# Layer 0's recurrence in seven small VectorE instructions a step instead of six, with the growth kept apart from its inverse

## The chip, the cores and the metric

The kernel runs on one core of a Trainium2 chip. The metric is the device time of one execution in microseconds. All data is float32.

## What is computed

The kernel computes a four-layer model on x of 8 sequences of 512 tokens and 256 channels. Of it, only the first part matters here. Layer 0 normalises x, forms keys, values and gates by three projections, and runs a recurrence over the 512 tokens for each of 8 x 256 channels:

```
def step(carry, kv_t):
    aa, bb, pp = carry
    kk, vv = kv_t
    uu_kk = u + kk
    p = jnp.maximum(pp, uu_kk)
    e1 = jnp.exp(pp - p)
    e2 = jnp.exp(uu_kk - p)
    y = (e1 * aa + e2 * vv) / (e1 * bb + e2)
    ...
    pp_n = pu + jnp.log(bb_n)
```

Beside it stands a mixture of 16 experts on the same normalised x: every expert's output, silu(gate) times up, projected down, is weighted by a router's column and added to the residual. The recurrence's denominators depend on the step before; the experts depend on nothing in it.

## The kernel before

The program is a sequence of blocks, each with one instruction stream for every engine and a barrier at its ends. Layer 0 has three: `layer0_project`, `layer0_experts` and `layer0_mix`.

`layer0_project` goes over the 8 sequences: normalisation, projections, routing, the shared expert. ScalarE writes the exponentials of the decays into `scan`, a tile that stays for all of layer 0. It has T + 2 places of time, two slots each, and 16 columns (two channel blocks times 8 sequences). Slot 0 of place t+1 first holds a decay d and is overwritten in the recurrence by the state q; slot 1 of place t+1 holds the inverse of a clamped ratio of the step before.

`layer0_experts` runs two things on the same engines at once. The experts' work is cut into 128 units, 16 experts times 8 sequences. For a unit TensorE multiplies up (`ps_gu`, L577), ScalarE forms `silu_g` (L564) and copies `up_rows` (L565), GpSimd multiplies the two into `hidden` (L553), TensorE multiplies down (`ps_y`, L586), and VectorE adds `ps_y`, times the column of `comb`, to the residual `x_res` (`combine`, L507). `ps_gu`, `hidden` and `ps_y` have two buffers each. TensorE's order is up of unit m+1, then down of unit m; the down waits for `hidden_ready` and for `y_free`, which VectorE's last half combine of two units before raises.

VectorE's stream interleaves the recurrence with the combines, four time steps a unit. A step before is: `recurrence` (L487), one SCALAR_TENSOR_TENSOR over both slots, new = (q + 1) * (d, inverse); the first half combine of a tile, 128 columns; a wait; the clamp of the ratio (L494, TENSOR_SCALAR); the product that writes q (L495); the second half combine; a wait; the reciprocal of the ratio into slot 1 of place t+2 (L501); a wait for that reciprocal. The semaphore `step` counts all four. The first combine of a unit waits for `down_done`. The units go as two without a combine, seven passes of a loop over `j` with 16 units written out in each (addresses of `scan` are computed in registers there), and a last 14 units with fixed addresses. In the profile the time of L487, L494, L495, L501 and L507 is that of these instructions, and the same lines under DVEq are register work of VectorE's sequencer.

`layer0_mix` reads q of all steps out of `scan`, with the time as the running index: `q_at` in GpSimd's two additions (L678, L679) and VectorE's product (L700).

Of the kernel before, what the change touches and what calls it, by code (L numbers as in the profile page):

```python
# [20 lines left out]
ALU = mybir.AluOpType  # L21
# [3 lines left out]
P = 128  # L25
B, T, D = 8, 512, 256
KD = D // P
# [3 lines left out]
ONE = 1  # L31
# [136 lines left out]
RATIO_MAX = 1e24  # L168


def layer0_project(nc, io, keep):


    with ExitStack() as stack:
# [85 lines left out]
        def _(dve):  # L260
# [5 lines left out]
            nc.vector.memset(scan[:, 0, 0, :], 0.0).then_inc(setup_done, 1)  # L266
            nc.vector.memset(scan[:, 1, 1, :], 1.0).then_inc(setup_done, 1)
# [63 lines left out]
        def _(act):  # L331
            act.wait_ge(cols_in, ONE + DMA)
            act.wait_ge(setup_done, ONE + 5)
# [30 lines left out]
            def decays(i):  # L364
                act.wait_ge(dk_ready, ONE + i + 1)
                for k in range(KD):
                    last = nc.scalar.activation(
                        scan[:, 1:T + 1, 0, bass.ds(B * k + i, 1)].rearrange("p t a -> p (t a)"), dk[:, k, :],
                        ACT.Exp, bias=cols[:, k, 3:4])
                last.then_inc(decayed, 1)  # L370
# [10 lines left out]
        def _(pe):  # L381
            pe.wait_ge(weights_in, ONE + 5 * DMA)
            pe.wait_ge(setup_done, ONE + 5)
# [58 lines left out]
def layer0_experts(nc, io, keep):  # L442
# [3 lines left out]
    with ExitStack() as stack:  # L446
# [8 lines left out]
        ratio = room.sb("ratio", KD * B)  # L455
# [8 lines left out]
        step = room.sem("step")  # L464
# [16 lines left out]
        def _(dve):  # L481
            dve.sem_inc(y_free, 2)

            def recurrence(t):


                nc.vector.scalar_tensor_tensor(  # L487
                    out=new[:], in0=scan[:, bass.ds(t, 1), 0, :].broadcast_to([P, 2, KD * B]), scalar=1.0,
                    in1=scan[:, bass.ds(t + 1, 1), :, :].rearrange("p a s c -> p (a s) c"),
                    op0=ALU.add, op1=ALU.mult).then_inc(step, 1)  # L490

            def recurrence_close(t):
                dve.wait_ge(step, ONE + 4 * t + 1)
                nc.vector.tensor_scalar(ratio[:], new[:, 0, :], 1.0, RATIO_MAX, ALU.max, ALU.min).then_inc(step, 1)  # L494
                nc.vector.scalar_tensor_tensor(  # L495
                    out=scan[:, bass.ds(t + 1, 1), 0, :].rearrange("p a c -> p (a c)"), in0=new[:, 0, :],
                    scalar=RATIO_MAX, in1=new[:, 1, :], op0=ALU.min, op1=ALU.mult).then_inc(step, 1)

            def recurrence_invert(t):
                dve.wait_ge(step, ONE + 4 * t + 3)  # L500
                nc.vector.reciprocal(scan[:, bass.ds(t + 2, 1), 1, :].rearrange("p a c -> p (a c)"),  # L501
                                     ratio[:]).then_inc(step, 1)
# [9 lines left out]
            def unit(j, m, with_sum):  # L512


                u = 2 * B * j + m
                for s in range(UNIT_STEPS):
                    t = UNIT_STEPS * u + s
                    recurrence(t)
                    if with_sum:
                        if s == 0:  # L520
                            dve.wait_ge(down_done, ONE + u + 1)
                        combine(m - 2, s, 2 * j + (m - 2) // B, 0)
                    recurrence_close(t)
                    if with_sum:
                        last = combine(m - 2, s, 2 * j + (m - 2) // B, 1)
                        if s == UNIT_STEPS - 1:
                            last.then_inc(y_free, 1)
                    recurrence_invert(t)
                    dve.wait_ge(step, ONE + 4 * t + 4)
# [78 lines left out]
def layer0_mix(nc, io, keep):  # L608
# [4 lines left out]
    with ExitStack() as stack:  # L613
# [38 lines left out]
        def q_at(i, k, first):  # L652
            return scan[:, first:first + T, 0, bass.ds(B * k + i, 1)].rearrange("p t a -> p (t a)")
# [2800 lines left out]
def build_program(nc, io):  # L3454
    with ExitStack() as stack:
# [9 lines left out]
        with ExitStack() as layer0:  # L3465
            room0 = Room(nc, layer0, "l0")
            keep.scan = room0.sb("scan", T + 2, 2, KD * B)
# [152 lines left out]
```

## Time and profile before

| | us |
|---|---|
| median of 3 timed runs | 4336.93 (4331.45 to 4337.49) |
| the profiled execution, its own time | 4330.87 |
| its span | 4329.1 |
| VectorE busy in the span | 2632.6 (61%) |
| TensorE busy in the span | 3557.8 (82%) |
| GpSimd busy in the span | 1320.7 (31%) |

The span is what lies between the first and the last instruction of the profiled execution. `layer0_experts` runs from about 199 to 973 us of it. Times below are counted from the span's start. In a timeline row come the start in us, the duration in us, the engine (DVE is VectorE, PE TensorE, ACT ScalarE, POOL GpSimd), the line and operation, what is written from what, the shape, the number of instructions merged, and in brackets the engine's idle time before it with what ended that.

### The profile page before, as it was taken

What the parts mean: (1) busy time and instruction counts of PE and PEld (TensorE: products, weight loads), DVE (VectorE), ACT (ScalarE), POOL (GpSimd) and SP (SyncE); (2) the same over time, 40 slices, a digit from 0 to 9 for tenths busy, and PEclk for the clock granted to TensorE, in tenths of its full rate; (3) what the DMA queues carried; (4) which work ended last, traced back from release to release, by engine and by line L of the source; (5) the groups of instructions that cost most, each with busy time, mean ns of one, the idle gap of its engine ahead of it and who ended that gap; (6) DMA issues with size and microseconds to landing.
All of it is one profiled execution on the core that took longest, in us unless ns stands there. A gap on an engine that the chain in (4) does not pass through costs nothing. (4 is left out here: it accounts for less than half of the span.)

```text
span 4329.1 us, 49464 instructions
## 1 busy us (share of the span) xinstructions
PE 3557.8 (82%) x15062; PEld 2035.1 (47%) x15062; DVE 2632.6 (61%) x6864; ACT 1266.9 (29%) x2471; POOL 1320.7 (31%) x787
## 2 busy tenths in 40 slices
PE   7898899895887999799999996899968745666665
PEld 4454555453564555444444454656544522333332
DVE  5588888898883444346666644122234537887885
ACT  4511111112223666244344432123213311111110
POOL 1021222221111544112112111320230038777872
PEclk9999999997998999999999987799979976777777
DMA  3100000001102000100000002122210010000000
GB/s 104 71 8 8 8 12 8 8 4 66 44 29 100 1 1 1 35 6 16 16 15 16 15 20 105 56 71 88 88 59 15 15 50 14 10 10 15 10 5 39
DMA packets 66796, 136.42 MB, mean 32 GB/s; under 512 B 8096, under 2 KB 40480, under 8 KB 65824
## 3 DMA queue, kind: packets, MB, share of 16 engines
q1 hardware_dynamic: 60448, 117.22, 8.0%
q0 software_dynamic: 6144, 16.79, 1.2%
q8 instruction: 91, 1.49, 0.1%
q14 instruction: 113, 0.93, 0.1%
HBM read 77.62 MB, written 56.36 MB: 31 GB/s over the span
## 5 line engine op out<-in xcount | busy, mean ns | idle before, releaser
L577 PE MATMUL p_ps_gu<-l0x_xnT_all,p_w 128*128 128x512 f32 x1024 | 465.3, 598 | 6.5 <-DMA p_w<-l_w 6.5
L507 DVE SCALAR_TENSOR_TENSOR all_x_res<-p_ps_y,l_comb,all_x_res 128x128 f32<-128x128 f32 (+1 forms) x1016 | 351.7, 347 | 12.6 <-PE p_ps_y L586 8.6
L553 POOL TENSOR_TENSOR p_hidden<-p_silu_g,p_up_rows 128x512 f32<-128x512 f32 x128 | 162.6, 1270 | 637.3 <-ACT p_up_rows L565 637.3
L1916 DVE CUSTOM_DVE_ANT_0 a_ps_s<-a_ps_s,a_hide_row,a_fmax 128x384 f32<-128x384 f32 (+3 forms) x512 | 249.3, 554 | 170.3 <-PE a_ps_s L1623 170.0
L586 PE MATMUL p_ps_y<-p_w,p_hidden 128*128 128x256 f32 x1024 | 257.2, 395 | 72.6 <-DVE all_x_res L507 72.4
L3134 POOL TENSOR_TENSOR b_prod<-b_q,b_kv 128x4096 f32<-128x4096 f32 x32 | 287.3, 9001 | 64.4 <-ACT b_kv L3328 50.2
L577 PEld LDWEIGHTS p_ps_gu<-l0x_xnT_all,p_w 128*128 128x128 f32 x1024 | 197.2, 193 | 201.1 <-issue 187.1
L3147 POOL TENSOR_TENSOR b_prod<-b_att,b_kv 128x4096 f32<-128x4096 f32 x32 | 281.4, 8806 | 16.7 <-ACT b_att L3338 12.1
L586 PEld LDWEIGHTS p_ps_y<-p_w,p_hidden 128*128 128x128 f32 x1024 | 190.4, 194 | 186.5 <-issue 132.1
L564 ACT ACTIVATE p_silu_g<-p_ps_gu 128x512 f32<-128x512 f32 x128 | 76.4, 597 | 613.2 <-PE p_ps_gu L577 613.2
L1828 POOL TENSOR_SCALAR_AFFINE_SELECT a_probs<-a_probs 128x512 f32<-128x512 f32 x128 | 79.9, 636 | 565.3 <-ACT a_probs L2105 565.3
L1124 POOL TENSOR_TENSOR a_probs<-a_probs,a_causal 128x512 f32<-128x512 f32 (+1 forms) x96 | 157.6, 1653 | 215.7 <-ACT a_probs L1353 215.7
L1353 ACT ACTIVATE a_probs<-a_ps_s 128x512 f32<-128x512 f32 (+1 forms) x384 | 170.7, 537 | 119.9 <-PE a_ps_s L993 119.9
L2105 ACT ACTIVATE a_probs<-a_ps_s 128x512 f32<-128x512 f32 (+1 forms) x384 | 171.8, 537 | 91.0 <-PE a_ps_s L1645 90.5
L487 DVE SCALAR_TENSOR_TENSOR p_new<-l_scan 128x32 f32 (+1 forms) x512 | 127.0, 248 | 101.8 <-DVE l_scan L501 31.4
L3436 PE MATMUL b_ps_kv<-b_w_e,b_hT 128*128 128x512 f32 x256 | 132.7, 651 | 57.3 <-DVE all_x_res L3276 57.3
L3436 PE MATMUL b_ps_e<-b_w_e,b_hT 128*128 128x512 f32 x256 | 146.7, 726 | 19.6 <-DVE all_x_res L3276 16.5
L494 DVE TENSOR_SCALAR p_ratio<-p_new 128x16 f32<-128x16 f32 x512 | 154.5, 302 | 1.8
L3178 DVE TENSOR_REDUCE b_att<-b_prod 128x256 f32<-128x4096 f32 x32 | 140.5, 4410 | 17.8 <-POOL b_prod L3134 17.8
L2307 PE MATMUL b_ps_y<-b_w_ff,b_gelu 128*128 128x256 f32 x512 | 123.4, 395 | 31.3 <-issue 30.3
L3191 DVE TENSOR_REDUCE b_y<-b_prod 128x256 f32<-128x4096 f32 x32 | 140.1, 4398 | 9.4 <-POOL b_prod L3147 9.4
L2295 PE MATMUL b_side<-b_hT,b_w_ff 128*128 128x512 f32 x256 | 128.9, 657 | 15.0 <-issue 13.1
(419 smaller groups left out, 7175.8 us busy)
## 6 DMA issues: line engine op xcount, KB each, us to landing
sorted_scratch<-all_zero SPq DMA_DIRECT2D x1, 9088.0 KB, 30.5
b_sorted_in<-sorted_scratch SPq DMA_DIRECT2D x17, 512.0 KB, 4.6
y_scratch<-b_y_out SPq DMA_DIRECT2D x17, 512.0 KB, 3.2
all_x_res<-x SPq DMA_DIRECT2D x8, 512.0 KB, 4.7
xn_scratch<-p_xn SPq DMA_DIRECT2D x8, 512.0 KB, 5.2
v_scratch<-p_v_sb SPq DMA_DIRECT2D x8, 512.0 KB, 2.6
r_scratch<-p_r_sb SPq DMA_DIRECT2D x8, 512.0 KB, 2.8
p_w<-l_w SPq DMA_DIRECT2D x16, 256.0 KB, 2.6
```

The costliest lines, as they stand in the source:

```text
L494: nc.vector.tensor_scalar(ratio[:], new[:, 0, :], 1.0, RATIO_MAX, ALU.max, ALU.min).then_inc(step, 1)
L507: return nc.vector.scalar_tensor_tensor(out=xb, in0=ps_y[m % 2][:, t, part], scalar=comb[:, TT * (m % B) + t, bass.ds(e, 1)], in1=xb, op0= ...
L553: nc.gpsimd.tensor_tensor(hidden[m % 2][:], silu_g[m % 2][:], up_rows[m % 2][:], ALU.mult).then_inc(hidden_ready, 1)
L577: last = nc.tensor.matmul(ps_gu[m % 2][:, half, :], w13[n][:, k, half * INTER0:(half + 1) * INTER0], xnT_all[:, k, (m % B) * T:(m % B + 1) ...
L586: last = nc.tensor.matmul(ps_y[m % 2][:, t, :], hidden[m % 2][:, t * P:(t + 1) * P], w2[n][:], start=True, stop=True)
L1124: nc.gpsimd.tensor_tensor(lead, lead, allowed, ALU.mult).then_inc(masked, 1)
L1353: nc.scalar.activation(probs[g % 2][:, j, T * part:T * part + PART_LEN[part]], ps_s[:, j, 0:PART_LEN[part]], ACT.Square, scale=HD ** -0.5) ...
L1916: last = nc.vector.tensor_tensor_reduce(out=there, in0=there, in1=hide_row[:, (TT - 1 - t) * P:], scale=HD ** -0.5, scalar=fmax[i % 2][:, ...
L2105: nc.scalar.activation(probs[:, j, T * part:T * part + PART_LEN[part]], ps_s[:, j, 0:PART_LEN[part]], ACT.Exp, scale=HD ** -0.5).then_inc( ...
L3134: nc.gpsimd.tensor_tensor(prod[t % 3][:].rearrange("p (h g d) -> p h g d", h=HEADS, g=HEADS), q[:, t, :].rearrange("p (h a d) -> p h a d", ...
L3147: nc.gpsimd.tensor_tensor(prod[(TT + t) % 3][:].rearrange("p (h d g) -> p h d g", h=HEADS, d=HD), att[:, t, :].rearrange("p (h a g) -> p h ...
L3436: last = nc.tensor.matmul(ps_e[n % 4][:], hT[1][:, k, t * P:(t + 1) * P], w_e[:, k, 2 * pair * D:2 * (pair + 1) * D], start=(k == 0), stop ...
```

## The change

The clamped ratio and slot 1 of `scan` go. `scan` has one slot a place, T + 1 places. Two small tiles take the rest: `new` keeps the growth and the numerator's partner, `share` keeps the growth's inverse and a bounded share. A step becomes: `grow` with two 16-wide SCALAR_TENSOR_TENSORs, new0 = (q + 1) * d and new1 = min(share0, 1) + share1; the first half combine; a wait for both; the reciprocal of new0 into share0; share1 = min(new0, 1) * new1; q = min(new0, RATIO_MAX) * new1; the second half combine; a wait for all five. The description also names GpSimd as keeper of the gate times up product; that product is GpSimd's in the kernel before and the diff doesn't touch it.

```diff
-            nc.vector.memset(scan[:, 0, 0, :], 0.0).then_inc(setup_done, 1)
-            nc.vector.memset(scan[:, 1, 1, :], 1.0).then_inc(setup_done, 1)
+            nc.vector.memset(scan[:, 0, :], 0.0).then_inc(setup_done, 1)
...
                     last = nc.scalar.activation(
-                        scan[:, 1:T + 1, 0, bass.ds(B * k + i, 1)].rearrange("p t a -> p (t a)"), dk[:, k, :],
+                        scan[:, 1:T + 1, bass.ds(B * k + i, 1)].rearrange("p t a -> p (t a)"), dk[:, k, :],
...
         new = room.sb("new", 2, KD * B)
-        ratio = room.sb("ratio", KD * B)
+        share = room.sb("share", 2, KD * B)
...
             dve.sem_inc(y_free, 2)
-
-            def recurrence(t):
-
-
+            nc.vector.memset(share[:, 0, :], 1.0).then_inc(share_set, 1)
+            nc.vector.memset(share[:, 1, :], 0.0).then_inc(share_set, 1)
+            dve.wait_ge(share_set, ONE + 2)
+
+            def grow(t):
+
+                q = scan[:, bass.ds(t, 1), :].rearrange("p a c -> p (a c)")
+                nc.vector.scalar_tensor_tensor(out=new[:, 0, :], in0=q, scalar=1.0,
+                                               in1=scan[:, bass.ds(t + 1, 1), :].rearrange("p a c -> p (a c)"),
+                                               op0=ALU.add, op1=ALU.mult).then_inc(step, 1)
+                nc.vector.scalar_tensor_tensor(out=new[:, 1, :], in0=share[:, 0, :], scalar=1.0, in1=share[:, 1, :],
+                                               op0=ALU.min, op1=ALU.add).then_inc(step, 1)
+
+            def settle(t):
+                dve.wait_ge(step, ONE + 5 * t + 2)
+                nc.vector.reciprocal(share[:, 0, :], new[:, 0, :]).then_inc(step, 1)
+                nc.vector.scalar_tensor_tensor(out=share[:, 1, :], in0=new[:, 0, :], scalar=1.0, in1=new[:, 1, :],
+                                               op0=ALU.min, op1=ALU.mult).then_inc(step, 1)
                 nc.vector.scalar_tensor_tensor(
-                    out=new[:], in0=scan[:, bass.ds(t, 1), 0, :].broadcast_to([P, 2, KD * B]), scalar=1.0,
-                    in1=scan[:, bass.ds(t + 1, 1), :, :].rearrange("p a s c -> p (a s) c"),
-                    op0=ALU.add, op1=ALU.mult).then_inc(step, 1)
-
-            def recurrence_close(t):
-                dve.wait_ge(step, ONE + 4 * t + 1)
-                nc.vector.tensor_scalar(ratio[:], new[:, 0, :], 1.0, RATIO_MAX, ALU.max, ALU.min).then_inc(step, 1)
-                nc.vector.scalar_tensor_tensor(
-                    out=scan[:, bass.ds(t + 1, 1), 0, :].rearrange("p a c -> p (a c)"), in0=new[:, 0, :],
+                    out=scan[:, bass.ds(t + 1, 1), :].rearrange("p a c -> p (a c)"), in0=new[:, 0, :],
                     scalar=RATIO_MAX, in1=new[:, 1, :], op0=ALU.min, op1=ALU.mult).then_inc(step, 1)
-
-            def recurrence_invert(t):
-                dve.wait_ge(step, ONE + 4 * t + 3)
-                nc.vector.reciprocal(scan[:, bass.ds(t + 2, 1), 1, :].rearrange("p a c -> p (a c)"),
-                                     ratio[:]).then_inc(step, 1)
...
                     t = UNIT_STEPS * u + s
-                    recurrence(t)
+                    grow(t)
                     if with_sum:
                         if s == 0:
                             dve.wait_ge(down_done, ONE + u + 1)
                         combine(m - 2, s, 2 * j + (m - 2) // B, 0)
-                    recurrence_close(t)
+                    settle(t)
                     if with_sum:
                         last = combine(m - 2, s, 2 * j + (m - 2) // B, 1)
                         if s == UNIT_STEPS - 1:
                             last.then_inc(y_free, 1)
-                    recurrence_invert(t)
-                    dve.wait_ge(step, ONE + 4 * t + 4)
+                    dve.wait_ge(step, ONE + 5 * t + 5)
...
         def q_at(i, k, first):
-            return scan[:, first:first + T, 0, bass.ds(B * k + i, 1)].rearrange("p t a -> p (t a)")
+            return scan[:, first:first + T, bass.ds(B * k + i, 1)].rearrange("p t a -> p (t a)")
...
-            keep.scan = room0.sb("scan", T + 2, 2, KD * B)
+            keep.scan = room0.sb("scan", T + 1, KD * B)
```

In `layer0_project` ScalarE and TensorE wait for four set-up steps instead of five.

## Rows read from the trace of the kernel before

**Rows 1.** Windows: busy us (x instructions) of PE, PEld, DVE, ACT, POOL; clock; DMA

```profile
600.00:700.00 100.00, 89.66 (x264) 49.56 (x263) 83.87 (x397) 19.53 (x35) 20.44 (x17) 0.98 0.03 9
```

**Rows 2.** Waits of TensorE and VectorE, 206 to 970 us: total, times, longest

```profile
PE p_ps_y L586 <- DVE all_x_res L507: 72.4, 91, 3.3
...
DVE all_x_res L507 <- PE p_ps_y L586: 6.5, 1, 6.5
```

**Rows 3.** Timeline of VectorE: the first instruction of two passes of the loop

```profile
605.57 0.19 DVE L487 SCALAR_TENSOR_TENSOR p_new<-l_scan 128x32 f32 x1 [3.12 <-issue]
...
702.59 0.19 DVE L487 SCALAR_TENSOR_TENSOR p_new<-l_scan 128x32 f32 x1 [3.12 <-issue]
```

**Rows 4.** Timeline of GpSimd, early in that pass

```profile
624.60 1.26 POOL L553 TENSOR_TENSOR p_hidden<-p_silu_g,p_up_rows 128x512 f32<-128x512 f32 x1 [3.89 <-ACT p_up_rows L565]
629.76 1.26 POOL L553 TENSOR_TENSOR p_hidden<-p_silu_g,p_up_rows 128x512 f32<-128x512 f32 x1 [3.90 <-ACT p_up_rows L565]
```

**Rows 5.** Timeline of VectorE: the last step of a unit and the next unit's start

```profile
655.68 0.24 DVE L501 RECIPROCAL l_scan<-p_ratio 128x16 f32 x1
656.07 0.19 DVE L487 SCALAR_TENSOR_TENSOR p_new<-l_scan 128x32 f32 x1
656.21 0.35 DVE L507 SCALAR_TENSOR_TENSOR all_x_res<-p_ps_y,l_comb,all_x_res 128x128 f32<-128x128 f32 x1
656.48 0.16 DVE L494 TENSOR_SCALAR p_ratio<-p_new 128x16 f32<-128x16 f32 x1
656.55 0.17 DVE L495 SCALAR_TENSOR_TENSOR l_scan<-p_new 128x16 f32 x1
656.64 0.34 DVE L507 SCALAR_TENSOR_TENSOR all_x_res<-p_ps_y,l_comb,all_x_res 128x128 f32<-128x128 f32 x1
656.90 0.24 DVE L501 RECIPROCAL l_scan<-p_ratio 128x16 f32 x1
657.41 0.19 DVE L487 SCALAR_TENSOR_TENSOR p_new<-l_scan 128x32 f32 x1 [0.27 <-DVE l_scan L501]
657.64 0.35 DVE L507 SCALAR_TENSOR_TENSOR all_x_res<-p_ps_y,l_comb,all_x_res 128x128 f32<-128x128 f32 x1
```

**Rows 6.** Register work of VectorE's sequencer, from lines' own views: ns min/median/max

```profile
L487 DVEq FUSED_REGOPS  x553: 53/53/110, 206.2 to 892.7; - x185
...
L507 DVEq FUSED_REGOPS  x448: 57/65/65, 212.9 to 892.8; - x150
```

**Rows 7.** Timeline of GpSimd and of VectorE at one product

```profile
646.12 1.27 POOL L553 TENSOR_TENSOR p_hidden<-p_silu_g,p_up_rows 128x512 f32<-128x512 f32 x1 [4.30 <-ACT p_up_rows L565]
...
646.70 0.74 DVE L487 SCALAR_TENSOR_TENSOR p_new<-l_scan 128x32 f32 x1
```

**Rows 8.** The page's costliest groups: busy us, mean ns of one

```profile
L487 DVE SCALAR_TENSOR_TENSOR p_new<-l_scan 128x32 f32 (+1 forms) x512 | 127.0, 248 | 101.8 <-DVE l_scan L501 31.4
L494 DVE TENSOR_SCALAR p_ratio<-p_new 128x16 f32<-128x16 f32 x512 | 154.5, 302 | 1.8
```

**Rows 9.** The same lines and L495 by duration: ns min/median/max

```profile
L487 DVE SCALAR_TENSOR_TENSOR p_new<-l_scan x512: 191/191/1298, 199.6 to 966.7; 128x32 f32 x149, 128x32 f32<-128x32 f32 x22
...
L494 DVE TENSOR_SCALAR p_ratio<-p_new x512: 156/164/1255, 199.8 to 967.1; 128x16 f32<-128x16 f32 x171
...
L495 DVE SCALAR_TENSOR_TENSOR l_scan<-p_new x512: 159/167/1266, 199.9 to 967.2; 128x16 f32 x149, 128x16 f32<-128x16 f32 x22
```

**Rows 10.** Timeline of VectorE in the last 14 units, with fixed addresses

```profile
940.41 0.19 DVE L487 SCALAR_TENSOR_TENSOR p_new<-l_scan 128x32 f32<-128x32 f32 x1
...
941.20 0.24 DVE L501 RECIPROCAL l_scan<-p_ratio 128x16 f32<-128x16 f32 x1
941.48 0.19 DVE L487 SCALAR_TENSOR_TENSOR p_new<-l_scan 128x32 f32<-128x32 f32 x1
```

**Rows 11.** VectorE on 512-wide operands, strided (L700) and packed (L1168): ns min/median/max

```profile
L700 DVE TENSOR_TENSOR p_inv<-p_inv,l_scan x16: 1019/1052/1091, 989.4 to 1272.7; 128x512 f32<-128x512 f32 x16
...
L1168 DVE SCALAR_TENSOR_TENSOR a_centred<-a_sums,a_side x32: 686/686/689, 1355.1 to 1683.0; 128x512 f32<-128x512 f32 x32
```

More of the change, by code:

```diff
@@ L332, in _ @@
             act.wait_ge(cols_in, ONE + DMA)
-            act.wait_ge(setup_done, ONE + 5)
+            act.wait_ge(setup_done, ONE + 4)
             def rows_turned(i):
@@ L382, in _ @@
             pe.wait_ge(weights_in, ONE + 5 * DMA)
-            pe.wait_ge(setup_done, ONE + 5)
+            pe.wait_ge(setup_done, ONE + 4)
             def turn_rows(i):
@@ L463, in layer0_experts @@
         down_done = room.sem("down_done")
-        step = room.sem("step")
+        step, share_set = room.sem("step"), room.sem("share_set")
         block = room.block()
```

## The prediction

> **What bounds the kernel now.** One core runs a sequence of blocks; the diff touches only layer 0, above all `layer0_experts`. So I first read the windows [rows 1]: in 600 to 700 us VectorE is busy 84 of 100 us and TensorE 90, so both are near full and neither alone is shown to be the bound. The waits decide [rows 2]: over the whole stage TensorE waited 72.4 us, 91 times, for VectorE's last combine of a unit (`y_free`), while VectorE waited for TensorE's `ps_y` once, at the very start. VectorE sets the pace. Its own timeline gives that pace: two passes of its loop over `j` start 702.59 - 605.57 = 97.0 us apart, and each starts behind 3.12 us in which VectorE does nothing, its jump back to the loop's head [rows 3]. That leaves (97.0 - 3.12)/16 = 5.87 us a unit.
>
> TensorE's own pace is seen early in a pass, where VectorE is still a unit's buffer ahead of needing it: GpSimd's products, one a unit, then come 629.76 - 624.60 = 5.16 us apart [rows 4]. A pass at TensorE's pace would be 16 x 5.16 = 82.6 us. The 14.4 us between 97.0 and 82.6, seven times over, is all that any edit of VectorE's loop can win: 101 us.
>
> **A unit of VectorE, taken apart.** Starts, not durations, count, because consecutive instructions overlap [rows 5]: grow (L487) to half combine 0.14, to clamp (L494) 0.27, to product (L495) 0.07, to half combine 0.09, to reciprocal (L501) 0.26, to the next grow 0.39. The sum is 1.22 us. The last term is the one with a bare wait: the reciprocal lasts 0.24, and behind it come the semaphore and 53 ns or more of register work for the dynamic addresses of `scan` [rows 6]. The edge of a unit adds 0.12 at the wait (0.51 for 0.39) and 0.09 at the wait for `down_done` (0.23 for 0.14): 0.21.
>
> The rest is a hold. Once a unit GpSimd multiplies 128x512 for 1.27 us, and the first L487, L494 or L495 that starts inside it ends only when it ends: the grow of 646.70 took 0.74 us instead of 0.19, GpSimd's product ran from 646.12 to 647.39 [rows 7]. In total L487 lost 127.0 - 512 x 0.191 = 29 us, L494 154.5 - 512 x 0.164 = 71 us [rows 8, 9]; L495, with one hold or a few (its longest is 1266 ns), some 4 us by an estimate from its mean. That is 104/128 = 0.81 us a unit. The steps are left with (5.87 - 0.21 - 0.81)/4 = 1.21 us each, as the row's 1.22 has it; I use 1.21.
>
> **The change part by part.**
> - *Taken away a step:* the 32-wide grow (0.14), the clamp (0.07), the reciprocal's exposed end (0.39).
> - *Added a step:* two 16-wide grows, a share product; the reciprocal moves behind the first half combine. Seven instructions for six. A 16-wide SCALAR_TENSOR_TENSOR releases the next start after 0.09, as L495 does [rows 5]; three new ones of that kind, and the old product, give 0.36. The two half combines give 0.26 to 0.27 each.
> - *The reciprocal with nothing waiting on it* is not in the trace. Every other instruction releases the next one about 0.08 before its own end (0.17 long, 0.09 to the next start; 0.34 long, 0.26) [rows 5], so 0.24 - 0.08 = 0.16. Bounds: 0.09, as a plain 16-wide operation, and 0.27, fully exposed as in the last pass without register work (941.20 to 941.48) [rows 10]. I take 0.16, by the nearest rows.
> - *The waits.* The wait before the reciprocal asks for the second grow, which is over 0.17 after its start, while the combine between them covers 0.26. The wait at the step's end now asks for the product, and a half combine stands behind that product: the product is over 0.08 after the combine starts, plus some 0.04 of semaphore, 53 ns of registers and 0.05 to reach the engine is 0.22, under 0.26. So I cost it at nothing; its cover is that half combine, with 0.04 to spare, and if the cover were too short the price is up to 0.39 - 0.27 = 0.12 a step. What is queued behind this wait is the next grow, then everything on VectorE, then TensorE by `y_free`.
> - *Register work* of 57 to 65 ns for the combine's `comb` column [rows 6] comes behind the second, short grow; only 0.09 covers it besides. I add 0.04, between 0 and 0.11 (what register work adds to a bare wait: 0.39 for 0.27 or 0.28 [rows 5, 10]).
> - *New step:* 0.09 + 0.09 + 0.04 + 0.26 + 0.16 + 0.09 + 0.09 + 0.26 = 1.08 us, 0.13 to 0.14 less than 1.21. *New edge:* 0.16 for 0.21, since the wait's register work at the edge starts earlier.
> - *The hold* stays: the clamp is gone, but the product, the share product and both grows read two tensors of SBUF like L487 and L495, which were held. Exposed starts now lie 0.09, 0.51, 0.09 and 0.35 apart, before 0.41, 0.07 and 0.74, so a product of GpSimd finds one a little sooner; against that, VectorE will at times be waiting at `down_done` anyway. I keep 0.81, between 0.2 (the product falls into that wait) and 1.2 (it is met at once).
> - *Unit:* 4 x 1.08 + 0.16 + 0.81 = 5.29, minus 5.87 is -0.58, to -0.61 with the step unrounded. *Pass:* 16 x 0.6 = 9.6 us. Seven passes: 67 us.
> - *Last pass, static addresses:* a step is 1.07 (940.41 to 941.48) [rows 10] and becomes 1.04; 14 units of four steps lose 14 x 4 x 0.03 = 1.7 us at most, and I take 1, since TensorE's pace is near. The first eight steps, without combine, have one exposed wait less; I take 0.5 us, between nothing and 8 x 0.14. One wait and two memsets more at the start, one memset less in the projection: under 0.5 us.
> - *Layout:* `scan` has a step of 64 bytes instead of 128. ScalarE's decays and the mix's reads stay strided. The mix's strided product takes 1.052 us [rows 11], a 512-wide operation with packed operands 0.686 [rows 11]; if the shorter step were as good as packed, 16 x 0.37 = 6 us would come off, which I take as nothing and keep for the range.
>
> Sum: 67 + 1 + 0.5 = about 69 us, with the upper rounding 72. The profiled execution took 4330.87 us; its own forecast is 4260. The three timed runs have a median of 4336.93, 6 us more; carried over, 4266. I forecast **4265 us**.
>
> **Against the row a rule.** The rows show instructions overlapping: L494 lasts 0.16 and L495 starts 0.07 behind it [rows 5]. The Trainium skill, VectorE: DVE Perf Modes, "The DRAIN you can't avoid" and "Rules for kernel authors", says that the next operation does not start until the pipe has emptied, that a semaphore costs nothing extra, and that one should "Minimize op *count*, not sems". By it this change, one operation more and a wait fewer, should lose; the sum above goes by the rows, which don't bear it out for independent neighbours.
>
> **The rivals.**
> - *VectorE paces, shorter unit* (the forecast): 4252 to 4285. Chance 0.60.
> - *TensorE paces.* If a unit falls below (82.6 - 3.12)/16 = 4.97, the jump's 3.12 us is made good within a pass and the pass is 82.6: 101 us and 2 more, 4337 - 103 = 4234. It needs the hold to shrink to 0.5 or less, because the product falls into VectorE's wait at `down_done`, or because only the clamp was really open to it. For the second speaks that the clamp took 71 of 104 us; against it, that L487 and L495 were held for up to 1298 and 1266 ns [rows 9]. The Trainium skill, SBUF — State Buffer, "Who interferes with whom", has operations with two SBUF inputs contending with a GpSimd operation that reads SBUF; the trace agrees, by those two maxima. Chance 0.14.
> - *The hold grows.* TensorE's next product is timed from VectorE's own release, so the phase can lock where each GpSimd product is met at its start: a unit is 4 x 1.08 + 0.16 + 1.2 = 5.68, a pass 3 us shorter, 21 + 1.5 in all: 4314. Half way: 4290. Chance for this side 0.17.
> - *The end wait stays bare* (the change doesn't do what it says): 0.12 more a step, a unit 5.77, 1.6 us a pass, 11 us: 4325. Chance 0.05.
> - *Slower.* One more instruction with nothing hidden: two grows at 0.14 each, 0.27, reciprocal 0.27, 0.09, 0.09, and 0.39 at the end make 1.39 a step, 0.17 to 0.18 over 1.21. On 448 steps in the passes that is 78 us: 4415. It decides from 0.14 a step above my sum, where the gain is gone. For it: the sequencer has more instructions to hand over in less time. Against: the reciprocal's wait and register work are hidden today behind a half combine, which releases it after 0.26, no later than the other half releases the clamp (0.27) [rows 5]. Chance 0.04.
>
> **How the numbers follow.** The time is that of the likeliest case. The range reaches to TensorE's pace below, 4234, and above to past the half-way point of the growing hold, 4303; outside lie the worst lock, the bare wait and the slow case, with nearly 0.2. 0.2%, about what a measurement of this kernel can tell from no change, is 8.7 us: faster 0.93, same 0.03, slower 0.04.
>
> **What would show it.** VectorE's starts of two passes 86 to 88 us apart; a step of 1.04 to 1.10 between two first grows in the middle of a unit; second half combine to next grow at 0.26; reciprocal to share product at 0.16; holds on the 16-wide SCALAR_TENSOR_TENSORs, on the reciprocals none; TensorE's wait for the combine down from 72.4 to some 20 us, nearly all of it behind VectorE's jumps; nothing changed from the mix on. Wrong if the step is over 1.15, if the holds' sum moves far from 104 us, or if TensorE never waits.

## The result, and the profile after

The changed kernel takes 4231.91 us (median of 4 runs, 4223.55 to 4235.75), the kernel before beside it 4335.1 us. The ratio is 0.976, 95% interval 0.9743 to 0.9778: 103 us less, where 70 were forecast. The time lies 2 us below the forecast's range and near the 4234 us of its second case, TensorE pacing. The profiled execution took 4229.58 us, with a span of 4227.9.

The block below is `layer0_experts`. The waits of VectorE and of TensorE from 200 to 890 us show who leads now; they answer to [rows 2]. A row has the total in us, the times and the longest.

```profile
DVE all_x_res L507 <- PE p_ps_y L585: 71.5, 65, 7.5
DVE p_new L489 <- issue: 17.8, 6, 3.2
...
PE p_ps_gu L576 <- DMA p_w<-l_w: 6.5, 1, 6.5
PE p_ps_y L585 <- POOL p_hidden L552: 0.8, 1, 0.8
```

TensorE, which waited 72.4 us for VectorE's combines, no longer waits for them at all. VectorE waits 71.5 us for TensorE's products. The parts have changed places. TensorE's timeline is then a plain alternation of up products (`ps_gu`, of the next unit) and down products (`ps_y`):

```profile
505.79 1.89 PE L585 MATMUL p_ps_y<-p_w,p_hidden 128*128 128x256 f32 x8
507.51 3.60 PE L576 MATMUL p_ps_gu<-l0x_xnT_all,p_w 128*128 128x512 f32 x8
510.95 1.89 PE L585 MATMUL p_ps_y<-p_w,p_hidden 128*128 128x256 f32 x8
512.67 3.60 PE L576 MATMUL p_ps_gu<-l0x_xnT_all,p_w 128*128 128x512 f32 x8
```

Down products follow each other after 510.95 - 505.79 = 5.16 us, the pace that [rows 4] showed early in a pass. In the windows (busy us of PE, PEld, DVE, ACT, POOL, then clock and DMA), which answer to [rows 1], TensorE is busy all of the 100 us:

```profile
600.00:700.00 100.00, 100.00 (x311) 58.86 (x310) 89.67 (x540) 22.99 (x40) 25.57 (x20) 1.00 0.03 9
```

Two passes of VectorE's loop start 545.52 - 462.96 = 82.56 us apart, against 97.0 in [rows 3], with much the same idle jump at their head, which now costs nothing. That is one distance of five in each trace; their means are 97.7 us before (97.0 to 98.7, so that [rows 3] show the shortest) and 82.6 now:

```profile
462.96 0.17 DVE L489 SCALAR_TENSOR_TENSOR p_new<-l_scan 128x16 f32 x1 [2.91 <-issue]
...
545.52 0.17 DVE L489 SCALAR_TENSOR_TENSOR p_new<-l_scan 128x16 f32 x1 [2.91 <-issue]
```

And one step in the middle of a unit, from VectorE's timeline, which answers to [rows 5]:

```profile
509.25 0.16 DVE L489 SCALAR_TENSOR_TENSOR p_new<-l_scan 128x16 f32 x1
509.34 0.16 DVE L492 SCALAR_TENSOR_TENSOR p_new<-p_share 128x16 f32<-128x16 f32 x1
509.42 0.34 DVE L507 SCALAR_TENSOR_TENSOR all_x_res<-p_ps_y,l_comb,all_x_res 128x128 f32<-128x128 f32 x1
509.68 0.23 DVE L497 RECIPROCAL p_share<-p_new 128x16 f32<-128x16 f32 x1
509.84 0.10 DVE L498 SCALAR_TENSOR_TENSOR p_share<-p_new 128x16 f32<-128x16 f32 x1
509.87 0.15 DVE L500 SCALAR_TENSOR_TENSOR l_scan<-p_new 128x16 f32 x1
509.95 0.34 DVE L507 SCALAR_TENSOR_TENSOR all_x_res<-p_ps_y,l_comb,all_x_res 128x128 f32<-128x128 f32 x1
510.21 0.16 DVE L489 SCALAR_TENSOR_TENSOR p_new<-l_scan 128x16 f32 x1
```

Starts: 0.09, 0.08, 0.26, 0.16, 0.03, 0.08, 0.26: 0.96 us for a step of seven instructions, where six took 1.21.

From the first combine to the last, the block goes from 213.1-973.2 us to 213.7-868.2 us of the span, 760.1 to 654.5. What lies behind it did not shrink: 3356 us and 3360, and 3349 in a second profile of the changed kernel (e5). So the gain is in this block. The span shrank by 101 us and the block by 106; the difference is smaller than that between the two profiles of the one kernel.

### The profile page after: what moved, and what is told of

It is laid out like the page before. It is cut to its first block and busy times, and to the rows that moved or that the text cites. A ratio compares the mean times of both kernels' runs of the same rounds, so it can differ in the third digit from the quotient of the medians.

```text
span 4227.9 us, 49083 instructions
## 1 busy us (share of the span) xinstructions
PE 3524.3 (83%) x15062; PEld 2036.9 (48%) x15062; DVE 2547.0 (60%) x7377; ACT 1267.0 (30%) x2471; POOL 1320.0 (31%) x787
## 5 line engine op out<-in xcount | busy, mean ns | idle before, releaser
L507 DVE SCALAR_TENSOR_TENSOR all_x_res<-p_ps_y,l_comb,all_x_res 128x128 f32<-128x128 f32 (+1 forms) x1016 | 347.3, 342 | 73.4 <-PE p_ps_y L585 71.5
L585 PE MATMUL p_ps_y<-p_w,p_hidden 128*128 128x256 f32 x1024 | 242.0, 379 | 0.8 <-POOL p_hidden L552 0.8
L2483 POOL DMA_INDIRECT b_rows<-y_scratch,b_slot_int x64 | 61.7, 964 | 254.5 <-issue 239.9
L2354 PE MATMUL b_side<-b_w_expert,b_sortedT 128*128 x284 | 135.5, 600 | 0.3 <-ACT b_sortedT L2733 0.3
```

Source lines behind the costliest of these rows:

```text
L507: return nc.vector.scalar_tensor_tensor(out=xb, in0=ps_y[m % 2][:, t, part], scalar=comb[:, TT * (m % B) + t, bass.ds(e, 1)], in1=xb, op0= ...
L585: last = nc.tensor.matmul(ps_y[m % 2][:, t, :], hidden[m % 2][:, t * P:(t + 1) * P], w2[n][:], start=True, stop=True)
```

## Experiments

The prediction left two questions. Which part of the edit carries the gain: the covered wait, or the smaller instructions and their holds? And why was it 103 and not 70? The theory after the result: VectorE's unit fell under the pace that lets it make good its jump, so that the block runs at TensorE's 5.16 us; below that point more speed on VectorE is worth nothing, and just above it the holds come back. The rival is that VectorE's work counts one for one and the step simply was shorter than I made it.

All numbers stand in this table, ahead of the single runs. "Block" is from the first combine's start to the last one's end, "pass" the distance of two passes of VectorE's loop, "holds" the time that the recurrence's instructions, and the spare ones of e4, e6 and e10, lasted beyond their line's median, each from the profiled execution. A pass is one distance of five; the five lie within 2 us of each other in every kernel, in e9 within 3.9 (83.8 to 87.7).

| kernel | ratio to before (95%) | median us | before beside it | block us | pass us | holds us |
|---|---|---|---|---|---|---|
| before | | | | 760.1 | 97.0 | 104 |
| changed | 0.976 (0.9743-0.9778) | 4231.91 | 4335.1 | 654.5 | 82.6 | 59 |
| e1 end wait bare | 0.9968 (0.9956-0.998) | 4264.79 | 4277.74 | 742.9 | 95.1 | 92 |
| e2 before, reciprocal covered | 0.9887 (0.987-0.9904) | 4231.14 | 4277.74 | 715.2 | 92.4 | 94 |
| e3 before, short GpSimd product | 0.9795 (0.9779-0.9811) | 4188.55 | 4277.74 | 669.5 | 85.6 | 2 |
| e4 changed, two spare operations | 0.9886 (0.9863-0.9909) | 4223.85 | 4277.74 | 709.8 | 89.9 | 105 |
| e5 changed again | 0.9748 (0.9734-0.9762) | 4217.39 | 4328.36 | 654.5 | 82.5 | 56 |
| e6 changed, one spare operation | 0.9808 (0.9794-0.9821) | 4243.21 | 4328.36 | 680.5 | 86.8 | 105 |
| e7 changed, no share product | 0.9761 (0.9748-0.9775) | 4220.98 | 4328.36 | 654.5 | 82.4 | 19 |
| e8 weights early | 0.9745 (0.9725-0.9764) | 4219.36 | 4328.36 | 654.5 | 82.5 | 58 |
| e9 reciprocal last | 0.9798 (0.9779-0.9817) | 4255.56 | 4342.59 | 673.5 | 86.4 | 106 |
| e10 one spare, short product | 0.9749 (0.9729-0.9769) | 4233.02 | 4342.59 | 653.5 | 82.9 | 1 |
| e11 weights early, later | 0.9739 (0.9724-0.9754) | 4231.63 | 4342.59 | 654.5 | 82.5 | 62 |

The runs came in three sets, each on a chip of its own and with the kernel before beside it. In the first set (e1 to e4) that kernel took 4277.74 us. The part behind the block is shorter there: in e1 it is 4263.6 - 961.6 = 3302 us, against 3356. So ratios and blocks are compared across sets, and medians only within one.

**e1: the end wait made bare.** The second half combine stands ahead of the reciprocal; the seven instructions are the same.

```diff
-                    settle(t)
                     if with_sum:
                         last = combine(m - 2, s, 2 * j + (m - 2) // B, 1)
                         if s == UNIT_STEPS - 1:
                             last.then_inc(y_free, 1)
+                    settle(t)
                     dve.wait_ge(step, ONE + 5 * t + 5)
```

> The changed kernel with the second half combine moved ahead of the reciprocal, so that nothing stands behind the q product and the wait at the step's end is bare. Same seven instructions. Theory (the cover of the end wait is what carried the gain): q product to next grow goes from 0.08 + 0.26 with the combine between to about 0.32 bare, while the combine's 0.26 moves elsewhere; the step rises from 0.95 to 1.18 us, a unit to 4 x 1.18 + 0.2 + 0.8 = 5.7, a pass from 82.6 to about 94.5 us, VectorE paces again: 4232 + 7 x 12 = 4316 us. Rival (the gain came from the clamp's removal and its holds alone): still TensorE-paced, 4232 to 4240 us.

VectorE's waits and TensorE's:

```profile
DVE p_new L489 <- DVE l_scan L500: 82.0, 435, 0.4
...
PE p_ps_y L585 <- DVE all_x_res L507: 48.6, 82, 3.7
```

The first row is the price laid open: in 435 steps the next grow waits for the q product, a row that the changed kernel has once, with 0.4 us. The pass is 95.1 us, the expectation 94.5. With the smaller instructions alone the block keeps 760.1 - 742.9 = 17 us of its 106: the order of the same instructions is worth 88. The bare wait itself, in one step:

```profile
625.61 0.16 DVE L500 SCALAR_TENSOR_TENSOR l_scan<-p_new 128x16 f32 x1
625.93 0.17 DVE L489 SCALAR_TENSOR_TENSOR p_new<-l_scan 128x16 f32 x1 [0.16 <-DVE l_scan L500]
```

From the q product to the next grow is 0.32 us, where 0.08 passed before the next instruction could start in the covered order. VectorE leads again (TensorE waits 48.6 us for it), and the holds are 92 us instead of 59.

**e2: the cover alone.** The kernel before, with its clamp and its six instructions, but the reciprocal ahead of the second half combine.

```diff
-                dve.wait_ge(step, ONE + 4 * t + 3)
+                dve.wait_ge(step, ONE + 4 * t + 2)
...
                     recurrence_close(t)
+                    recurrence_invert(t)
                     if with_sum:
...
-                    recurrence_invert(t)
                     dve.wait_ge(step, ONE + 4 * t + 4)
```

> The kernel before, six instructions with the clamp kept, but the reciprocal issued ahead of the second half combine, so that the combine covers the reciprocal's end. Theory: the end wait drops from 0.39 to 0.26 but the reciprocal now waits for the clamp, some 0.33 us after the clamp's start where the next start came after 0.16; a step goes from 1.21 to about 1.16, a unit from 5.87 to 5.6 or 5.5, a pass from 97.0 to 92 or 93: 4335 - 30 = 4305 us, with the clamp's holds as before (0.5 to 0.8 us a unit). Rival (the wait alone was the whole cost): TensorE-paced, about 4235 us. Second rival (reordering within six instructions gains nothing): 4335 us.

```profile
500.78 0.17 DVE L494 TENSOR_SCALAR p_ratio<-p_new 128x16 f32<-128x16 f32 x1
500.85 0.17 DVE L495 SCALAR_TENSOR_TENSOR l_scan<-p_new 128x16 f32 x1
501.11 0.25 DVE L501 RECIPROCAL l_scan<-p_ratio 128x16 f32 x1
501.28 0.26 DVE L507 SCALAR_TENSOR_TENSOR all_x_res<-p_ps_y,l_comb,all_x_res 128x128 f32<-128x128 f32 x1
501.51 0.19 DVE L487 SCALAR_TENSOR_TENSOR p_new<-l_scan 128x32 f32 x1
```

The timeline of VectorE shows both sides of the trade: combine to next grow is 0.23, but clamp to reciprocal is 501.11 - 500.78 = 0.33, as expected, because the reciprocal needs the clamp's result. The median is 47 us lower, not the 30 expected, though the pass, 92.4 us, is the expected 92 to 93. The expectation counted from 97.0; the five distances have a mean of 97.7 before and 92.1 here, so that the seven passes give some 39 us of the block's 45, and the last 14 units the rest. So reordering alone has somewhat under half of the gain. The timelines place the rest in the chain: here the reciprocal must wait for the clamp and starts 0.26 behind the product of L495, while in the changed kernel no clamp stands between grow and reciprocal, and the two products follow the reciprocal after 0.16 and 0.03. No run tests that part by itself.

**e3: the holds alone.** The kernel before, GpSimd's product 32 columns wide. The other 15/16 of `hidden` is set to zero once, so most of the experts' sum is left out.

```diff
...
-                    nc.gpsimd.tensor_tensor(hidden[m % 2][:], silu_g[m % 2][:], up_rows[m % 2][:],
+                    nc.gpsimd.tensor_tensor(hidden[m % 2][:, 0:32], silu_g[m % 2][:, 0:32], up_rows[m % 2][:, 0:32],
```

> The kernel before with GpSimd's product of gate and up cut from 512 to 32 columns; 15/16 of hidden stays at zero, so the experts' sum is left out for most tokens. Theory (holds add to VectorE's unit): the product lasts 0.15 to 0.3 us, the holds fall from 104 us to under 25, a unit from 5.87 to 5.1 or 5.3, a pass from 97 to 84.5 to 88: 4335 - 7 x 11 = about 4258 us (4245 to 4275). Rival (TensorE's order, not the holds, sets the pace): 4325 to 4335 us.

The groups of VectorE's instructions (busy us, mean ns, idle us before) answer to [rows 8]:

```profile
L488 DVE SCALAR_TENSOR_TENSOR p_new<-l_scan 128x32 f32 (+1 forms) x512 | 99.7, 195 | 102.3 <-DVE l_scan L502 31.4 <-issue 20.0 <-PEq L49 2.4
...
L495 DVE TENSOR_SCALAR p_ratio<-p_new 128x16 f32<-128x16 f32 x512 | 85.0, 166 | 2.1
```

The grow's mean falls from 248 to 195 ns, the clamp's from 302 to 166. Nothing of the recurrence was touched, yet the block loses 91 us. The expectation's rival, that the holds don't set the pace, is out. In one pass nine of the sixteen units of VectorE last 5.07 to 5.09 us and the others up to 5.44; with the jump taken off, the mean is 5.15. That is about TensorE's own pace and not under 4.97, so the jump is not made good and the pass is 85.6. The order's 88 us (e1) and the holds' 91 don't add, because the floor gives 106 in all.

**e4, e6: work added to VectorE.** Two, or one, more 16-wide operations a step, with two SBUF inputs, on a tile that nothing reads.

```diff
...
+                for n in range(2):
+                    nc.vector.scalar_tensor_tensor(out=spare[:, n + 1, :], in0=spare[:, 0, :], scalar=1.0,
+                                                   in1=spare[:, 0, :], op0=ALU.min, op1=ALU.mult)
```

> The changed kernel with two more 16-wide operations with two SBUF inputs in every step, on a spare tile, between the q product and the second half combine; nothing reads them. 2 x 0.085 x 4 = 0.68 us more VectorE work a unit. Theory (TensorE paces as long as VectorE's unit with its holds is under 4.97 us): a unit without holds is 3.9 + 0.68 = 4.58, with holds of 0.5 to 0.9 it is 5.1 to 5.5, just over; a pass 85 to 91 us, the holds' sum back up from 60 to 90 us or more: 4250 to 4295 us, by the estimate of phases 4290. Rival (VectorE's work still counts one for one): 448 x 0.17 = 76 us, 4308 us. Rival (a full operation with its drain each, 0.165): 4380 us.

> The changed kernel with one more 16-wide operation with two SBUF inputs a step on a spare tile, between the q product and the second half combine: 0.34 us more VectorE work a unit. Theory (slack under TensorE's pace): a unit without holds is 4.24; with holds of 0.47 it is 4.71 and the time is that of the changed kernel, within 3 us; with holds back at 0.8 it is 5.05, a pass 84 to 85 us, up to 18 us more. Rival (one for one): 38 us more, and half the gap of the kernel with two such operations.

**e5: the changed kernel beside e6 to e8.**

> The changed kernel once more, to have its time beside the variants of this call. Theory (it is paced by TensorE): its gain over the kernel before is 103 us whatever the rest of the program takes; passes 82.6 us apart; against the first four runs, whose kernel before took 4278, it would be at 4175. Rival (the gain belongs to the rest of the program or to the chip): the gain differs by over 10 us.

The gain is 111 us there (0.9748, interval overlapping the first 0.976) and the block is the same, 654.5 us: a property of the block.

One spare operation costs 4243.21 - 4217.39 = 26 us, within one set; by the blocks of the two 26, too. That is more than the 18 I allowed and less than the 38 of one for one. Two cost 55 us of block against one for one 76. So neither reading is right by itself: part of the first operation falls into slack, and the holds return. From e6's groups:

```profile
L500 DVE SCALAR_TENSOR_TENSOR p_share<-p_new 128x16 f32<-128x16 f32 x504 | 105.4, 209 | 0.0
L502 DVE SCALAR_TENSOR_TENSOR l_scan<-p_new 128x16 f32 (+1 forms) x504 | 102.8, 204 | 0.0
```

(share product and q product, means 209 and 204 ns), and of the changed kernel, where L498 is the share product and L500 the q product, means 136 and 185:

```profile
L500 DVE SCALAR_TENSOR_TENSOR l_scan<-p_new 128x16 f32 (+1 forms) x504 | 93.4, 185 | 0.0
L498 DVE SCALAR_TENSOR_TENSOR p_share<-p_new 128x16 f32<-128x16 f32 x504 | 68.4, 136 | 0.0
```

And from e6's timeline two grows, one step apart in the middle of a unit, and a spare operation that is held like the others:

```profile
500.69 0.16 DVE L491 SCALAR_TENSOR_TENSOR p_new<-l_scan 128x16 f32 x1
...
501.73 0.16 DVE L491 SCALAR_TENSOR_TENSOR p_new<-l_scan 128x16 f32 x1
...
504.62 1.26 DVE L506 SCALAR_TENSOR_TENSOR p_spare<-p_spare 128x16 f32<-128x16 f32 x1
```

The holds, those of the spare operation among them, go from 56 to 105 us with one operation and stay at 105 with two. In the prediction's terms e6's unit is 4 x 1.04 + 0.16 = 4.32 without a hold: with the changed kernel's 56/128 = 0.44 it would be 4.76, under the 4.97 at which TensorE paces, and with the 105/128 = 0.82 measured it is 5.14, over it. e4 fell inside its range: 0.9886 of 4335 us is 4286, between 4250 and 4295, and its pass of 89.9 between 85 and 91.

**e10: the same spare operation without the holds.**

> The changed kernel with one spare operation a step, as in the earlier run that lost 26 us, and GpSimd's product cut to 32 columns (15/16 of hidden stays zero, most of the experts' sum is left out). Theory (the spare operation cost more than its own slack only because it put VectorE back in the lead, where a hold of 0.8 us a unit meets it): without holds a unit is 4.25 us, far under 5.16, so TensorE paces, passes 82.6 us apart, a ratio to the kernel before of 0.975. Rival (the spare operation costs by itself): passes stay near 86.8 us, a ratio of 0.981.

```profile
DVE all_x_res L513 <- PE p_ps_y L594: 95.0, 107, 7.4
```

The ratio is 0.9749, the changed kernel's own, and VectorE waits 95 us for TensorE. The operation that cost 26 us costs nothing as soon as GpSimd's product is short. Its price was not its 0.08 us a step by itself: it had one only together with the holds, which are 1 us here. This run takes away all holds, not just those that came back in e6; that the returned ones carry the 26 us is the sum given above, not a measurement.

**e7: work taken from VectorE.** The share product is left out and share1 stays zero; a part of the recurrence is missing. The counts that the two waits ask for go down with it.

```diff
...
-                nc.vector.scalar_tensor_tensor(out=share[:, 1, :], in0=new[:, 0, :], scalar=1.0, in1=new[:, 1, :],
-                                               op0=ALU.min, op1=ALU.mult).then_inc(step, 1)
...
```

> The changed kernel without the share product: share1 stays at zero, so the recurrence's second factor is wrong by that part. Six instructions a step. Theory (TensorE paces): no change from the changed kernel, within 3 us, passes 82.6 us apart, only VectorE's wait for down_done grows. Rival (VectorE's instruction count still costs): 512 x 0.03 to 0.09 = 14 to 45 us less.

```profile
DVE all_x_res L505 <- PE p_ps_y L583: 152.4, 112, 7.9
```

4220.98 beside e5's 4217.39, within 3.6 us and the runs' spread; the block is 654.5 us in both. The 14 to 45 us of the rival don't appear. VectorE waits 152 us instead of 71.5. Under TensorE's pace an instruction less is worth nothing.

**e9: the reciprocal last.** It stands behind both products.

```diff
-                nc.vector.reciprocal(share[:, 0, :], new[:, 0, :]).then_inc(step, 1)
...
                     scalar=RATIO_MAX, in1=new[:, 1, :], op0=ALU.min, op1=ALU.mult).then_inc(step, 1)
+                nc.vector.reciprocal(share[:, 0, :], new[:, 0, :]).then_inc(step, 1)
```

> The changed kernel with the reciprocal behind the two products instead of ahead of them. In the changed kernel reciprocal to share product is 0.16 and share product to q product 0.03 us, 0.19 for both where two plain intervals would be 0.25. Theory (the reciprocal's long pass hides part of the operation behind it, and only the first of them): share product to q product goes to 0.08, q product to reciprocal 0.08, reciprocal to half combine 0.13 to 0.16; the step grows from 0.95 by 0.04 to 0.06, a unit by 0.2, still at or just under TensorE's pace with holds: 0 to 12 us over the changed kernel, a ratio to the kernel before of 0.975 to 0.978. Rival (0.03 belongs to the share product itself, whatever is ahead of it): share to q stays 0.03, the step unchanged.

```profile
500.76 0.17 DVE L497 SCALAR_TENSOR_TENSOR p_share<-p_new 128x16 f32<-128x16 f32 x1
500.85 0.17 DVE L499 SCALAR_TENSOR_TENSOR l_scan<-p_new 128x16 f32 x1
500.93 0.25 DVE L502 RECIPROCAL p_share<-p_new 128x16 f32<-128x16 f32 x1
501.09 0.26 DVE L507 SCALAR_TENSOR_TENSOR all_x_res<-p_ps_y,l_comb,all_x_res 128x128 f32<-128x128 f32 x1
```

The share product now lasts 0.17 and the q product starts 0.09 behind it, so the 0.03 was not the share product's own. In e7 the q product stands behind the reciprocal, and there it has the short record (a median of 0.106 us) and the short interval (0.028). Behind the reciprocal now stands a half combine, and it lasts 0.26 instead of 0.34, here and in e2. The mechanism is as expected, the price is not: 0.9798, about 20 us over the changed kernel where I allowed 12. The step grew by 0.05 or 0.06, to a median of 1.01, and the holds came back here too, to 106 us. By the prediction's formula a unit of 4 x 1.01 + 0.16 + 0.81 = 5.01 is just over 4.97, a pass 0.7 us longer and seven of them 5 us; the block is 19 us longer. Just above the point where the lead changes the formula gives too little (in e6 18 us for 26), well above it, it fits (e4: 4 x 1.12 + 0.16 + 0.81 = 5.45, a pass of 90.3 for 89.9). Why is open.

**e8, e11: TensorE's start.** The first two experts' weights are loaded in the projection's block: at its head (e8), or behind its loop (e11).

```diff
...
+            for e in range(2):
+                sp.dma_start(keep.w13[e][:], io.l0_w13[e:e + 1].rearrange("e p k n -> p (e k) n")).then_inc(experts_in, DMA)
+                sp.dma_start(keep.w2[e][:], io.l0_w2[e:e + 1].rearrange("e p d -> p (e d)")).then_inc(experts_in, DMA)
...
-            load(0, 0)
-            load(1, 1)
...
```

> The changed kernel with the first two experts' weights loaded during the projection, into tiles that live through both blocks, so that TensorE doesn't wait for them at the head of the experts' block (6.45 us idle there, of which some 3 lie behind the barrier). Theory (TensorE's order is now the chain of the whole block): its first product starts about 3 us sooner and so does everything behind it, 2 to 5 us less than the changed kernel, the only kind of edit in this block that still pays. Rival (VectorE or the table load of ScalarE holds the start anyway): the same time.

> The changed kernel with the first two experts' weights loaded in the projection's block behind its loop of loads, not at its head, where in the earlier run they delayed the first sequence by 14.4 us of waiting for w2s. Theory: the projection ends when it did, TensorE's idle stretch between the two blocks falls from 6.6 to some 3.8 us, and everything behind comes 3 us sooner; a ratio of 0.974 against 0.975, within what the runs can tell, so the trace decides: first down product near 208.5 instead of 211.4 us. Rival: the start of the block is held elsewhere and stays.

Neither is told from the changed kernel by time (0.9745 and 0.9739 against 0.9748), and e11's own sign, a first down product near 208.5 us, failed: it starts at 212.68. What the trace does show is a shorter stretch from the projection's last product of TensorE to the block's first down product. That is TensorE in e8:

```profile
198.10 1.99 PE L433 MATMUL p_ps_v<-p_w2s,p_hidden 128*128 128x256 f32 x8 [1.41 <-DVE p_hidden L317]
203.91 8.80 PE L580 MATMUL p_ps_gu<-l0x_xnT_all,l0x_w 128*128 128x512 f32 x16 [3.81 <-ACTq L561]
212.55 1.89 PE L589 MATMUL p_ps_y<-l0x_w,p_hidden 128*128 128x256 f32 x8
```

and in e5, the changed kernel:

```profile
194.03 1.99 PE L428 MATMUL p_ps_v<-p_w2s,p_hidden 128*128 128x256 f32 x8 [1.41 <-DVE p_hidden L312]
202.68 8.92 PE L576 MATMUL p_ps_gu<-l0x_xnT_all,p_w 128*128 128x512 f32 x16 [6.65 <-DMA p_w<-l_w]
211.43 1.89 PE L585 MATMUL p_ps_y<-p_w,p_hidden 128*128 128x256 f32 x8
```

14.45 us against 17.40; in e11 it is 212.68 - 197.00 = 15.68, since its first sixteen products took 10.04 us, at a mean granted clock of 0.66 in 206 to 210 us (0.96 in e5), a mix of its two levels, 0.5 and 1 (1.2 and 2.4 GHz). TensorE's idle time between the blocks falls from 6.65 us to 3.81 in both. So some 2 to 3 us are won in the stretch. They can't be seen in the whole because the projection's own end lies further apart: in the eleven profiles that leave these loads alone its last product starts between 193.7 and 200.6 us. The granted clock goes with it. Its mean over 30 to 190 us is 0.97 in the five profiles that end by 194.3 us (before, changed, e4, e5 and e6), 0.95 in e2 and e9 (198.2 and 197.9) and 0.93 in e1, e3, e7 and e10 (199.7 to 200.6); e8 and e11 have 0.95 and end at 198.1 and 197.0. What I wrote ahead of e11, that the head's loads in e8 had delayed the first sequence by 14.4 us, was wrong: the changed kernel waits 14.1 us there as well. e11 is nominally the fastest of all, by less than the runs can tell. What bounds the block now is TensorE's sixteen recorded products a unit, and no run here shortens those.

## Why the prediction was wrong

- **Who bounds the kernel before, and TensorE's pace of 5.16 us: right.** The pace was read from two rows of GpSimd, and it is the one at which the changed kernel runs throughout.
- **A unit taken apart into starts, edge and hold: right.** e3 removes the hold term alone, and the pass falls from 97.0 to 85.6. The terms without the hold give 5.05 us a unit; most of e3's last 5.07, their mean is 5.15.
- **The pass of 97.0: the shortest of five.** Their mean is 97.7, so what could be won was 7 x (97.7 - 82.6) = 106 us and not 101; the block lost 106.
- **The new step, "1.08": wrong, it measured 0.96.** This is the term that failed. Three pieces of it: the share product and the q product behind the reciprocal were put at 0.16 + 0.09 and take 0.16 + 0.03 (e9 shows that the short interval follows the reciprocal); the 0.04 for register work at the `comb` column didn't appear, grow to combine is 0.08; and the other intervals were each rounded up, 0.02 in all.
- **Its consequence.** With 0.96 the prediction's own formula gives 4 x 0.96 + 0.16 + 0.81 = 4.81, under the 4.97 below which "the jump's 3.12 us is made good within a pass", and the time of that case was 4234, 2 us from the result. That it is so close is partly luck: the block gave 106 us where that case has 103, and the rest of the program took the difference back. That case had a chance of 0.14, because I asked of it a shrinking hold and didn't put it to the step's own uncertainty; a step 0.08 shorter than my sum was enough. The bound for a term that decides between two cases has to be carried into their chances. The hold did fall, to 59/128 = 0.46 us a unit, but only with the shorter step: at a step of 1.04 (e6) it is back at 0.82, and at 1.12 (e4) the same.
- **Its own signs.** Three failed: passes of 86 to 88 us (82.6), a step of 1.04 to 1.10 (0.96), some 20 us of waits of TensorE (none). Two that it had named for being wrong came true: the holds' sum left 104 us, and TensorE never waits.
- **Had the step been 1.08,** the forecast would have been near. The runs with longer steps bear it out: e6, with a step of 1.04 (500.69 to 501.73 between two grows), has 0.9808 x 4335 = 4252 us; e4, with 1.12 (501.12 to 502.24), has 0.9886 x 4335 = 4286. On the line between them 1.08 is 4269; the forecast was 4265.
- **The end wait "at nothing": right.** Second half combine to next grow is 0.26 (509.95 to 510.21). At the edge of a unit it is 0.35 (507.21 to 507.56), and the wait for `down_done` adds 0.08 (503.64 to 503.80): 0.17 together, for 0.16 allowed. The bare price came out larger than the 0.12 a step I gave as its bound: the start after the q product moves from 0.08 to 0.32 in e1, 0.24 a step, and its order costs 88 us of block. I had priced a wait whose cover is too short by a little, not one without a cover.
- **The hold: kept, as forecast, on the SCALAR_TENSOR_TENSORs.** L489, L492, L498 and L500 reach 1260, 1245, 980 and 1260 ns, the reciprocal never more than 254. The clamp's share of 71 us went to the other lines where VectorE paces: e1, e4, e6 and e9, without a clamp, have 92 to 106 us. So its size, kept at 0.81 a unit, is about right there (e2: 94 us) and wrong under TensorE's pace (59 us, 0.46 a unit).
- **Against the rule.** One instruction more and a wait covered made the kernel faster by 103 us, and e1, with the same seven instructions and the wait bare, gives 88 us of that block back. The Trainium skill, VectorE: DVE Perf Modes, "Rules for kernel authors", asks for fewer operations, not fewer semaphores; for 16-wide operations with independent neighbours this trace does not agree. The prediction gave that page's "The DRAIN you can't avoid" by half: the same paragraph says that a next operation which is not held starts earlier. With that the trace agrees, as an operation of 0.165 us releases the next after 0.08.
- **Layout and the rest: right at nothing, nearly.** The mix's strided product went from a median of 1.052 us to 1.035, and behind the block stand 3360 us against 3356.

The coarse forecast held: a sure gain, and the clamp's removal alone wasn't its cause (17 us of block in e1).

## What to carry to other kernels

In an interleaved loop, first ask how much time the other engine's own pace leaves; then find the critical wait and put an independent instruction behind the producer that it waits for, even at the price of one more small instruction. Near the point where two engines change the lead, small terms decide by tens of microseconds: compute the threshold first, and give the chance of crossing it from the uncertainty of every term on the way. A hold by another engine was no constant of an instruction in these kernels; it went with who leads, 92 to 106 us where VectorE had little idle time, 56 to 62 where it waited 66 to 75 us for TensorE, and 19 where it waited 152.

## What the hardware showed that I had not expected

- An instruction right behind a 16-wide reciprocal has a record shorter by 0.06 to 0.08 us (0.11 for 0.17, 0.26 for 0.34), and behind a 16-wide one of these the next starts sooner (0.03 for 0.08 us).
- Holds go with the lead: with one operation of 0.08 us a step more, VectorE's holds rose from 56 to 105 us, and the kernel took 26 us longer; with GpSimd's product at 0.25 us instead of 1.27 the same operation was free.
- The projection, all but the same code in eleven profiles, ends between 193.7 and 200.6 us of the span, with the clock that TensorE was granted on the way (a mean of 0.97 in the early ones, 0.93 in the late). A gain of 2 to 3 us behind it needs the trace, from a point behind that difference.
